# Pair sums of weighed states on GpSimd in a fused two-layer kernel on one core

## The chip, the cores and the metric

The kernel runs on one core of a Trainium2 chip. The time is device microseconds (us) of one launch, as the median of several runs. A core has TensorE (matmuls into PSUM banks of 128 x 512 f32), VectorE, ScalarE (activation functions), GpSimd (which works on SBUF only here) and SyncE, which issues the DMAs. Each engine runs its own list of instructions in order and waits on semaphores that others raise.

## The reference

There are eight batches of 512 tokens x 256 features and two layers. The first layer (attention-like mixing and a mixture of experts) isn't touched by the change. The second layer is a Mamba-like state-space block and a gated MLP with ternary weights. What matters of it:

```python
raw, gate = split(x @ W_in)                    # 512 inner features each
h  = silu(causal_conv4(raw) + conv_b)
ts, B, C = split(h @ W_x, [64, 80])            # 16 values of B and of C per token
dt = softplus(ts @ W_dt + b_dt)
dA = exp(dt[..., None] * A)                    # 16 states n per feature
state = dA * state + dt * B * h                # along the 512 tokens
y  = sum over n of state[n] * C[n]             # the sum that the change touches
y  = (y + h * D) * silu(gate);  out = y @ W_out
# then the MLP: silu(x@w1)*(x@w2) -> gelu(@h1) -> gelu(@h2) -> @w3, 1024 wide
```

## The kernel before

Features lie over the 128 partitions, the 512 tokens along the free axis. A batch's inner features are 4 tiles (`KI`), worked off in two halves of 2 tiles (`HC`). For each half the 16 states n are gone through, and for each n both tiles: one step s handles one (n, tile) pair, 64 steps (`STEPS`) a batch. The four steps of two successive states are 2n, 2n+1 (state n, tiles 0 and 1) and the two behind them.

One step is this chain:

- SyncE brings the rows of B and C for state n into `bc`, spread over the partitions (L1165, one DMA of 512 KB for two steps, three buffers).
- ScalarE writes exp(dt * A) into a PSUM bank (L1251; three banks, `DEC`; it waits until the step three before has been weighed).
- GpSimd multiplies `u` = dt * h by the row of B into `d_in` (L1186, three buffers, `IN`).
- VectorE scans along the tokens in the PSUM bank (L1196, `scan`), and behind the next scan it multiplies the state by the row of C into `w_st` (L1204, `weigh`; three buffers, `WG`; it waits until the step three before has been summed).
- TensorE adds the weighed state to the output's bank with the identity as the other operand (L1271). f32 matmuls show as two records each. The bank was begun with h * D (L1263).

After a half's last step VectorE multiplies the bank by the gate (L1210, `gate_output`), then TensorE does `W_out` (L193) and VectorE adds the result to the tokens, through the tile `tokB` (L1235, L1238).

Three things run beside each other in a period: the core of batch b, the front of batch b+1 (norm L181, `W_in`, convolution taps L1020 and L1024 on `raw` and `cv`, SiLU, dt; `front_*`), and the MLP of batch b-1 (`mlp_*`). The MLP's activations are kept as a high part in fp32r and a low part: ScalarE writes the Gelu twice (L1456), GpSimd subtracts (L1373, `f0L`, `f1L`), TensorE multiplies both parts (L199, L200), and VectorE does the gating of the first layer (L1394, L1398). The weights come by DMA into `w_stage` and are cast by ScalarE into `w_ring` (L1427). Exp, Gelu and SiLU need different activation tables on ScalarE, and every change of table is an `ACT_TABLE_LOAD`.

The order on each engine is set when the program is built: each part is a generator that gives a planned time before each piece (`step_at(b, s)` is 2.8 planned us a step, with offsets from the table `PLAN`), and `in_order` takes the piece with the smallest one. These are places in an order and not measured times.

## Time and profile before

| | us |
|---|---|
| median of 3 runs (lowest to highest) | 2847.69 (2846.69 to 2848.17) |
| profiled execution | 2851.47 |
| its span in the profile | 2849.6 |

| engine | busy us | share of the span |
|---|---|---|
| TensorE (PE) | 2498.0 | 88% |
| VectorE (DVE) | 1770.3 | 62% |
| ScalarE (ACT) | 1453.9 | 51% |
| GpSimd (POOL) | 1093.9 | 38% |

The shares are of the whole span, of which the first layer fills somewhat less than the first 1100 us. The rows on which the prediction rests are cut by batches: the scans of the eight batches begin at 1159.8, 1315.8, 1517.3, 1720.6, 1926.9, 2129.1, 2331.0 and 2535.2 us, and the last one ends at 2704.8. PE's ends are modelled, so a busy PE isn't PE at its peak; PEld is the weight load, which overlaps the matmuls. A wait is named by the engine, its output tile and line, and behind the arrow by what ended it.

### The profile page before, as it was taken

To read this page: it belongs to the slowest core of one execution; us is meant where nothing else is said; L and a number is where in the kernel's file an instruction comes from. 1 tells how busy PE (TensorE), PEld (TensorE's weight loads), DVE (VectorE), ACT (ScalarE), POOL (GpSimd) and SP (SyncE) were. 2 spreads that over 40 slices of the span, in tenths; PEclk is the share of its full clock that TensorE was granted. 3 is DMA by queue.
4 is the path that set the end of the run, shared out by engine and by line. 5 is a ranking of instruction groups with operands and counts; after the bars stand their busy time and mean duration, and the time that the engine had idled before them with its cause. 6 is when DMAs were issued, how large, how long until landed. Compare 5 with 4: busy or idle time off the path is not lost.

```text
span 2849.6 us, 25916 instructions
## 1 busy us (share of the span) xinstructions
PE 2498.0 (88%) x8180; PEld 1510.3 (53%) x8180; DVE 1770.3 (62%) x2758; ACT 1453.9 (51%) x1938; POOL 1093.9 (38%) x841
## 2 busy tenths in 40 slices
PE   2899999999999997677898898898898897998977
PEld 1456555565656564223555465465564564565665
DVE  2544444444444423789968869869779679678630
ACT  0222322323222222554686786786776776867733
POOL 0220101202010100455655565565565556557622
PEclk6899999999999998788999999999999999999989
DMA  7000000000000000344464564564554554546622
GB/s 250 0 0 1 23 23 0 23 1 23 1 23 6 3 8 30 104 117 116 134 173 126 136 178 113 140 171 111 148 159 124 164 146 125 162 140 164 173 76 82
DMA packets 278665, 263.33 MB, mean 92 GB/s; under 512 B 15136, under 2 KB 209456, under 8 KB 278528
## 3 DMA queue, kind: packets, MB, share of 16 engines
q1 hardware_dynamic: 278528, 261.67, 32.9%
q8 instruction: 66, 1.08, 0.2%
q14 instruction: 71, 0.58, 0.1%
HBM read 252.61 MB, written 9.01 MB: 92 GB/s over the span
## 4 chain that ended last, share of the span: by engine, by line
PE 18%; DVE 12%; issue 10%; ACT 8%; DMA 7%; POOL 4%; SPq 1%; DVEq 0%; ACTq 0%; POOLq 0%
DMA w_stage<-h_T 6%; PE bank L1271 5%; PE bank L193 4%; DVE w_st L1204 3%; DVE bank L1196 3%; PE bank L199 3%; PE bank L200 3%; POOL d_in L1186 2%; ACT w_ring L1427 2%; ACT bank L1251 2%; DVE cv L1024 2%; ACT L1251 2%; PE bank L1504 1%; POOL f1L L1373 1%; PE bank L1505 1%
## 5 line engine op out<-in xcount | busy, mean ns | idle before, releaser
L1186 POOL TENSOR_TENSOR d_in<-u,bc 128x512 f32<-128x512 f32 x512 | 665.3, 1315 | 444.6 <-DMA bc<-bc_rows 318.8
L1196 DVE TENSOR_TENSOR_SCAN bank<-bank,d_in 128x512 f32<-128x512 f32 x512 | 624.7, 1221 | 188.0 <-ACT bank L1251 159.7
L1271 PE MATMUL bank<-w_st,ident 128*128 128x512 f32 x1024 | 542.6, 643 | 118.7 <-DVE w_st L1204 118.4
L1251 ACT ACTIVATE bank<-dt,a_neg 128x512 f32<-128x512 f32 x512 | 348.1, 687 | 300.0 <-DVE w_st L1204 298.5
L199 PE MATMUL bank<-f1H,w_ring 128*128 128x512 f32 x768 | 355.5, 463 | 39.4 <-POOL f1L L1373 26.4
L1271 PEld LDWEIGHTS bank<-w_st,ident 128*128 128x128 f32 x1024 | 194.3, 201 | 351.3 <-DVE w_st L1204 222.8
L1204 DVE TENSOR_TENSOR w_st<-bank,bc 128x512 f32<-128x512 f32 x512 | 344.1, 673 | 55.1 <-PE bank L1271 54.9
L200 PE MATMUL bank<-f1L,w_ring 128*128 128x512 f32 x768 | 312.6, 407 | 0.0
L748 DVE SCALAR_TENSOR_TENSOR f_both<-bank,rt,f_both 128x256 f32<-128x256 f32 x256 | 112.1, 480 | 303.9 <-PE bank L193 303.9
L176 POOL TENSOR_TENSOR norm_rstd<-norm_veps,minus_half 128x4 f32<-128x4 f32 x24 | 24.3, 1011 | 613.3 <-DVE norm_veps L172 613.3
L199 PE MATMUL bank<-f0H,w_ring 128*128 128x512 f32 x512 | 227.9, 445 | 10.8 <-POOL f0L L1373 5.6
L797 ACT ACTIVATE e_act<-bank 128x512 f32<-128x512 f32 x128 | 75.7, 597 | 315.0 <-PE bank L193 314.8
L1427 ACT ACTIVATE w_ring<-w_stage 128x1024 fp32r<-128x1024 f32 (+1 forms) x192 | 173.1, 906 | 113.9 <-DMA w_stage<-h_T 57.6
L193 PE MATMUL bank<-w_down,e_act 128*128 128x256 f32 x1024 | 230.2, 379 | 0.0
L193 PE MATMUL bank<-f_both,w_up 128*128 128x512 f32 x512 | 228.9, 592 | 0.0
L1373 POOL TENSOR_TENSOR f0L<-mid,f0H 128x512 fp32r<-128x512 f32 x128 | 170.8, 1336 | 136.6 <-ACT f0H L1456 79.5
L193 PEld LDWEIGHTS bank<-w_down,e_act 128*128 128x128 f32 x1024 | 194.6, 190 | 50.3 <-issue 25.1
L199 PEld LDWEIGHTS bank<-f1H,w_ring 128*128 128x128 f32 x768 | 151.7, 198 | 111.9 <-issue 44.1
L200 PE MATMUL bank<-f0L,w_ring 128*128 128x512 f32 x512 | 206.2, 403 | 0.0
L200 PEld LDWEIGHTS bank<-f1L,w_ring 128*128 128x128 f32 x768 | 151.7, 198 | 52.5 <-issue 23.5
L193 PEld LDWEIGHTS bank<-f_both,w_up 128*128 128x128 f32 x512 | 97.3, 190 | 101.5 <-issue 98.8
L1251 ACT ACT_TABLE_LOAD x115 | 147.5, 1283 | 2.0
(175 smaller groups left out, 3573.6 us busy)
## 6 DMA issues: line engine op xcount, KB each, us to landing
bc<-bc_rows SPq DMA_DIRECT2D x256, 512.0 KB, 5.1
w_stage<-h_T SPq DMA_DIRECT2D x256, 256.0 KB, 3.4
w_stage<-w_T SPq DMA_DIRECT2D x128, 128.0 KB, 3.2
xA<-L_attn_x SPq DMA_DIRECT2D x8, 512.0 KB, 4.0
x_mid<-xA SPq DMA_DIRECT2D x8, 512.0 KB, 2.9
xB<-x_mid SPq DMA_DIRECT2D x8, 512.0 KB, 5.0
xM<-x_mid SPq DMA_DIRECT2D x8, 512.0 KB, 8.0
x_out<-xM SPq DMA_DIRECT2D x8, 512.0 KB, 6.6
```

Source lines behind the costliest of these rows:

```text
L193: i = pe.matmul(out_, lhs(k), rhs(k), start=(k == 0), stop=(k == nk - 1))
L199: pe.matmul(out_, weights(k), hi(k), start=(k == 0), stop=False)
L200: i = pe.matmul(out_, weights(k), lo(k), start=False, stop=(k == nk - 1))
L748: i = dve.scalar_tensor_tensor(out=f[:, t, :], in0=bank[:, j * D:(j + 1) * D], scalar=r[:, 7, t, e:e + 1], in1=f[:, t, :], op0=ALU.mult, o ...
L797: act.activation(e_act[:, e % 2, m, :], bank[:, :], ACT.Gelu).then_inc(up_act.sem, 1)
L1186: pool.tensor_tensor(d_in[:, nth(b, s) % IN, :], u[:, c, :], rows_tile(b, use)[:, 0, :], ALU.mult).then_inc(in_made.sem, 1)
L1196: dve.tensor_tensor_scan(bank[:, :], bank[:, :], d_in[:, nth(b, s) % IN, :], 0.0, ALU.mult, ALU.add).then_inc(scanned.sem, 1)
L1204: dve.tensor_tensor(w_st[:, nth(b, s) % WG, :], state_bank(b, s)[:, :], rows_tile(b, step(s)[2])[:, 1, :], ALU.mult).then_inc(weighed.sem, 1)
L1251: act.activation(state_bank(b, s)[:, :], dt[:, c, :], ACT.Exp, scale=a_neg[:, c, n:n + 1]).then_inc(dA_made.sem, 1)
L1271: pe.matmul(y_bank(c)[:, :], ident[:, :], w_st[:, nth(b, s) % WG, :], start=False, stop=(n == NST - 1)).then_inc(summed.sem, 1)
L1373: pool.tensor_tensor(lo, f_full[:, i % 2, :], hi.bitcast(F32), ALU.subtract).then_inc(low_made.sem, 1)
L1427: act.activation(ring_part(w), stage_part(w), ACT.Copy).then_inc(ring_made.sem, 1)
```

## The change

For a step of an odd state n, GpSimd adds the tile of the state before (same feature tile) to this one's in place (`pairs_pool`, new signal `paired`), and TensorE sums only the result: 256 sums in place of 512. `w_st` has four buffers (`2 * HC`) in place of three. The weighing waits for `paired` in a step of an even state and for `summed` in one of an odd state. The tile `tokB` goes and its rows lie in the convolution's `raw`, so ScalarE's copy of the first channel waits for the end of the batch two before. The table `PLAN` has new numbers.

```diff
 PLAN = dict(
-    rows_out=106.9, norm_rstd=29, norm_stats=26, norm_apply=34.2, conv=45.7, raw_gap=11.7, tap_gap=3, u_first=136.5,
+    pair=4.8, rows_out=106.9, norm_rstd=29, norm_stats=24.1, norm_apply=34.5, conv=45.1, raw_gap=11.7, tap_gap=3.2,
...
-            tokB = sb("tokB", [P, 2, D])
...
+            tokB = raw[:, 0, PAD:].rearrange("p (t d) -> p t d", d=D)
...
-            BC, IN, WG, DEC = 3, 3, 3, 3
+            BC, IN, WG, DEC = 3, 3, 2 * HC, 3
...
+            def weighed_tile(b, s):
+                return w_st[:, nth(b, s) % WG, :]
+
+            def pair(s):
+                return s // (2 * HC) * HC + s % HC
...
                         act.wait_ge(*tap_made.at(b - 1, (c + 3) * KC))
+                        if b >= 2 and c == 0:
+                            act.wait_ge(*xM_made.all(b - 2))
...
+            def pairs_pool(b):
+                for s in range(STEPS):
+                    if step(s)[0] % 2:
+                        yield step_at(b, s) + PLAN["pair"]
+                        pool.wait_ge(*weighed.at(b, s + 1))
+                        pool.tensor_tensor(weighed_tile(b, s), weighed_tile(b, s), weighed_tile(b, s - HC), ALU.add
+                                           ).then_inc(paired.sem, 1)
...
                     if nth(b, s) >= WG:
                         before, old = step_back(b, s, WG)
-                        dve.wait_ge(*summed.at(before, old + 1))
-                    dve.tensor_tensor(w_st[:, nth(b, s) % WG, :], state_bank(b, s)[:, :], rows_tile(b, step(s)[2])[:, 1, :], ALU.mult
+                        freed = summed if step(s)[0] % 2 else paired
+                        dve.wait_ge(*freed.at(before, pair(old) + 1))
+                    dve.tensor_tensor(weighed_tile(b, s), state_bank(b, s)[:, :], rows_tile(b, step(s)[2])[:, 1, :], ALU.mult
                                       ).then_inc(weighed.sem, 1)
 
                 def gate_output(c):
-                    dve.wait_ge(*summed.at(b, (c // HC + 1) * HALF))
+                    dve.wait_ge(*summed.at(b, (c // HC + 1) * HALF // 2))
...
-                    pe.wait_ge(*weighed.at(b, s + 1))
-                    pe.matmul(y_bank(c)[:, :], ident[:, :], w_st[:, nth(b, s) % WG, :], start=False, stop=(n == NST - 1)
-                              ).then_inc(summed.sem, 1)
+                    if n % 2:
+                        pe.wait_ge(*paired.at(b, pair(s) + 1))
+                        pe.matmul(y_bank(c)[:, :], ident[:, :], weighed_tile(b, s), start=False, stop=(n == NST - 1)
+                                  ).then_inc(summed.sem, 1)
```

On GpSimd, in the full batch that the trace shows from 1720.6 us on, from step 42 to step 50 (`d_in` the product of each step, `f1L` and `f0L` the MLP's low halves), before:

```order
L1186 TENSOR_TENSOR d_in<-u,bc 128x512 x4
L1373 TENSOR_TENSOR f1L<-mid,f1H 128x512
L1186 TENSOR_TENSOR d_in<-u,bc 128x512
L1373 TENSOR_TENSOR f1L<-mid,f1H 128x512
L1186 TENSOR_TENSOR d_in<-u,bc 128x512 x4
L1373 TENSOR_TENSOR f0L<-mid,f0H 128x512
```

The same stretch of GpSimd now, steps 43 to 51 (`w_st<-w_st` is the addition):

```order
L1195 TENSOR_TENSOR d_in<-u,bc 128x512 x3
L1203 TENSOR_TENSOR w_st<-w_st 128x512
L1195 TENSOR_TENSOR d_in<-u,bc 128x512
L1203 TENSOR_TENSOR w_st<-w_st 128x512
L1392 TENSOR_TENSOR f1L<-mid,f1H 128x512
L1195 TENSOR_TENSOR d_in<-u,bc 128x512
L1392 TENSOR_TENSOR f1L<-mid,f1H 128x512
L1195 TENSOR_TENSOR d_in<-u,bc 128x512 x2
L1203 TENSOR_TENSOR w_st<-w_st 128x512
L1195 TENSOR_TENSOR d_in<-u,bc 128x512
L1203 TENSOR_TENSOR w_st<-w_st 128x512
L1195 TENSOR_TENSOR d_in<-u,bc 128x512
```

The addition of step s stands behind the product of step s+3, and the low halves are one step later than they were.

On TensorE, at that batch's end, where the output's bank is closed (the dt tiles of the next batch, then the last sums), before:

```order
L193 MATMUL bank<-xp,w_dt 128x512 x2
L1271 MATMUL bank<-w_st,ident 128x512 x3
L1504 MATMUL bank<-w,f0H 128x256
L1505 MATMUL bank<-w,f0L 128x256
L1504 MATMUL bank<-w,f0H 128x256
```

The same place on TensorE now:

```order
L193 MATMUL bank<-xp,w_dt 128x512 x2
L1290 MATMUL bank<-w_st,ident 128x512 x2
L1523 MATMUL bank<-w,f0H 128x256
L1524 MATMUL bank<-w,f0L 128x256
L1523 MATMUL bank<-w,f0H 128x256
```

Two sums stand between the dt tiles and the MLP's last products where there were three.

## Rows read from the trace of the kernel before

**Rows 1.** Busy us by stretch: PE, PEld, DVE, ACT, POOL, PEclk, DMA share, GB/s.

```profile
1160.00:1316.00 156.00, 111.83 (x192) 38.83 (x192) 138.46 (x166) 75.89 (x105) 87.33 (x67) 0.82 0.44 115
1721.00:1927.00 206.00, 180.36 (x619) 112.03 (x618) 163.81 (x204) 150.15 (x193) 118.09 (x92) 0.96 0.53 142
2535.00:2705.00 170.00, 155.56 (x549) 100.51 (x548) 135.88 (x170) 125.90 (x160) 108.03 (x86) 0.96 0.61 163
```

**Rows 2.** The same by stretches of one batch, and 21 steps of the last.

```profile
1720.60:1819.60 99.00, 79.44 (x279) 48.22 (x278) 96.29 (x128) 61.66 (x80) 54.20 (x41) 0.93 0.46 119
1819.60:1863.50 43.90, 41.59 (x135) 24.66 (x134) 24.80 (x30) 37.98 (x49) 22.55 (x18) 1.00 0.55 148
1863.50:1917.90 54.40, 50.63 (x177) 33.92 (x176) 39.38 (x45) 42.06 (x53) 35.65 (x30) 0.97 0.65 184
1917.90:1926.90 9.00, 9.00 (x36) 5.54 (x35) 3.63 (x7) 8.74 (x13) 5.70 (x5) 1.00 0.40 117
2649.10:2703.50 54.40, 50.97 (x178) 34.14 (x177) 37.30 (x43) 43.07 (x54) 35.45 (x29) 0.97 0.60 173
```

**Rows 3.** Waits of 1721 to 1927: total us, times, longest us.

```profile
POOL d_in L1186 <- DMA bc<-bc_rows: 39.5, 13, 5.6
...
DVE bank L1196 <- ACT bank L1251: 23.5, 9, 5.4
...
POOL f1L L1373 <- ACT f1H L1456: 14.6, 4, 5.2
...
DVE w_st L1204 <- PE bank L1271: 8.2, 6, 2.7
...
POOL f0L L1373 <- ACT f0H L1456: 7.1, 4, 3.4
...
DVE hcv L1210 <- PE bank L1271: 6.4, 2, 5.4
```

**Rows 4.** The chain that ended last, 1517 to 2535, shares by line.

```profile
by line: issue 17.0%; DMA w_stage<-h_T 10.5%; PE bank L1271 7.6%; DVE bank L1196 6.5%; DVE w_st L1204 6.3%; PE bank L199 5.1%; PE bank L193 4.9%; PE bank L200 4.9%; ACT bank L1251 3.2%; ACT L1251 2.9%; POOL d_in L1186 2.8%; ACT w_ring L1427
```

**Rows 5.** One piece of the chain in 1721 to 1927: start us, us.

```profile
1885.17 2.58 PE bank L1271 x6
```

**Rows 6.** Timeline at a batch's end: start us, us, then idle before it.

```profile
1922.80 2.84 PE L1271 MATMUL bank<-w_st,ident 128*128 128x512 f32 x6
...
1925.68 1.29 DVE L1210 TENSOR_TENSOR hcv<-bank,gate 128x512 f32<-128x512 f32 x2 [5.37 <-PE bank L1271]
```

**Rows 7.** Single lines over the whole run: ns least/median/most, first and last start.

```profile
L1024 DVE SCALAR_TENSOR_TENSOR cv<-raw,conv_w,cv x96: 729/750/1867, 1127.6 to 2435.3; 128x512 f32<-128x512 f32 x96
...
L1398 DVE CAST f0H<-mid x64: 404/450/1503, 1360.5 to 2753.5; 128x512 fp32r<-128x512 f32 x64
...
L181 DVE TENSOR_SCALAR cv<-xB,normB_stat,normB_rstd x32: 400/1348/1492, 1118.4 to 2372.0; 128x256 f32<-128x256 f32 x32
L181 DVE TENSOR_SCALAR mid<-xM,normM_stat,normM_rstd x32: 398/407/1368, 1339.5 to 2729.9; 128x256 f32<-128x256 f32 x32
...
L1196 DVE TENSOR_TENSOR_SCAN bank<-bank,d_in x512: 1205/1219/1232, 1159.8 to 2703.5; 128x512 f32<-128x512 f32 x171
...
L1204 DVE TENSOR_TENSOR w_st<-bank,bc x512: 665/673/694, 1162.1 to 2705.3; 128x512 f32<-128x512 f32 x171
...
L1186 POOL TENSOR_TENSOR d_in<-u,bc x512: 1254/1282/2239, 1158.5 to 2701.7; 128x512 f32<-128x512 f32 x171
...
L1251 ACT ACT_TABLE_LOAD  x115: 1283/1283/1283, 1155.9 to 2697.8; - x115
```

**Rows 8.** Groups of VectorE in 1721 to 1927: busy us, mean ns.

```profile
L1024 DVE SCALAR_TENSOR_TENSOR cv<-raw,conv_w,cv 128x512 f32<-128x512 f32 x12 | 12.6, 1048 | 0.0
L1398 DVE CAST f0H<-mid 128x512 fp32r<-128x512 f32 x8 | 6.3, 785 | 0.1
...
L181 DVE TENSOR_SCALAR cv<-xB,normB_stat,normB_rstd 128x256 f32<-128x256 f32 x4 | 4.4, 1151 | 0.0
L181 DVE TENSOR_SCALAR mid<-xM,normM_stat,normM_rstd 128x256 f32<-128x256 f32 x4 | 3.7, 976 | 0.0
```

More of the change, by code:

```diff
@@ L915, in adaln_kernel @@
             y_begun = signal("y_begun", KI)
-            dA_made, in_made, scanned, weighed, summed = (signal(n, STEPS) for n in
-                                                          ("dA_made", "in_made", "scanned", "weighed", "summed"))
+            dA_made, in_made, scanned, weighed = (signal(n, STEPS) for n in ("dA_made", "in_made", "scanned", "weighed"))
+            paired, summed = signal("paired", STEPS // 2), signal("summed", STEPS // 2)
             y_gated = signal("y_gated", KI)
@@ L1511, in adaln_kernel @@
                      *(mlp_sync(b) for b in every), *(out_sync(b) for b in every))
-            in_order(*(front_pool(b) for b in every), *(core_pool(b) for b in every), *(mlp_pool(b) for b in every))
+            in_order(*(front_pool(b) for b in every), *(core_pool(b) for b in every), *(pairs_pool(b) for b in every), *(mlp_pool(b) for b in every))
             in_order(*(front_scalar(b) for b in every), *(core_scalar(b) for b in every), *(weights_scalar(b) for b in every),
```

12 lines of the change are left out of this document (6 added, 6 removed).

## The prediction

> **What bounds the kernel now.** I read the busy times by stretch first, then the waits, then the chain, then single durations. The first layer holds none of the changed code. What the change can move are the eight state cores between 1160 and 2705 us: the first, 156 us, beside the second batch's front only, six full periods of about 203 us, (2535 - 1316) / 6, and the last, 170 us, with no front beside it [rows 1]. The 145 us behind them, to the span's 2849.6, are the last MLP, which the change leaves as it is.
>
> In a full period (206 us in the one shown) TensorE is busy 180.4 us, VectorE 163.8, ScalarE 150.2 and GpSimd 118.1. TensorE has the largest share, but the period is not one stage. Cut at scans 0, 30, 42 and 63 it reads [rows 2]: over the first 99 us VectorE is busy 96.3 and TensorE 79.4, so the first half of a batch, with norms, convolution and the gating of the MLP's first layer, is VectorE's. In the next 43.9 us TensorE has 41.6 and ScalarE 38.0 while VectorE has 24.8. In the 54.4 us after that TensorE shows 50.6 and ScalarE 42.1. But the last core, with less other work on TensorE before it, also takes 54.4 us for the same 21 states, so that stretch keeps a cadence of its own. It is the ring of exponentials (three PSUM banks) broken by ScalarE's Gelu groups: VectorE waits 23.5 us a batch for an exponential, against 8.2 us in the weighing for a sum by TensorE and 6.4 us in the gating of the output [rows 3]. The chain that ended last says the same of five periods (1018 us): the sums, L1271, hold 7.6% of it, and VectorE's scans and weighings 12.8% [rows 4].
>
> **The change part by part.**
>
> *TensorE loses every second sum.* 256 of 512 matmuls with the identity go. A matmul is two records; three of them took 2.84 us with the tail of the last, and 2.58 in the chain, so 0.86 us each [rows 5, 6]. That is 220 us of TensorE's time, 27.5 a batch. Only what VectorE waits for counts of it. The weighing L1204 waits 8.2 us a batch for one of three buffers. Now a buffer is one of four: an odd state's tile must be summed four states later, not three, and an even state's is freed by GpSimd and not by TensorE, which sits for two hidden tiles in a row. I let 7 of the 8.2 us go. At the batch's end VectorE waits 5.37 us before the gating while TensorE does two dt tiles and three sums [rows 6]; now there are two sums, 0.86 us less. With the 1.0 us at the first half's end (the rest of the 6.4) I take 2 us.
>
> *GpSimd gains 32 additions a batch.* The nearest row is its own product of the same shape, d_in, 1.28 us in the median [rows 7]: 41 us a batch, 118 to 159 of 203. The order puts the addition of state s behind d_in of s+3, two additions to four products. With nothing else to do, VectorE takes 1.22 + 0.67 us for a state, 7.6 for four [rows 7], and GpSimd 6 x 1.28 = 7.7: equal. In the cadence of scans 42 to 63, 2.6 us a state, GpSimd is busy 35.7 of 54.4 us; 10.5 additions make it 49. So it keeps up, but its stretches of waiting (39.5 us a batch for the row DMAs, 14.6 and 7.1 for the Gelu halves [rows 3]) shrink to a fifth of the time. The added wait is the weighing of an even state behind the addition of the state two before it. Behind that weighing on VectorE stand the next scan and everything else, and ScalarE's exponential three states on waits for it. Its slack is two states less the addition, some 2 us. I take 1 us a batch for it; below, 0, if GpSimd is always in time, and above, all that the first rival gives.
>
> *The additions get in VectorE's way.* Of VectorE's operations some stretch while GpSimd runs: the convolution's taps L1024 took 729 ns at least and 1867 at most, the cast L1398 404 to 1503, the normalisation L181 398 or 400 to 1368 and 1492, while the scan stayed within 1205 to 1232 and the weighing within 665 to 694 [rows 7]. In the period shown the excess over the shortest is 12 x 0.32 = 3.8 us for L1024, 4 x 0.75 + 4 x 0.58 = 5.3 for L181, 8 x 0.38 = 3.0 for L1398 [rows 7, 8], together 12.1 us, nearly all in the 99 us in which VectorE has no idle time to hide it. GpSimd is busy 54.2 of these 99 us [rows 2]; 15 additions are 19.2 us more, 35%. So 12.1 x 0.35 = +4.3 us a batch. Below it could be 0 (the additions fall beside scans), above 12.1 again if every one of them hits.
> By the Trainium skill (GPSIMD Engine Reference, Key points) GpSimd shares its SBUF interfaces with VectorE and contends with VectorE instructions that run in a two-port mode or have two SBUF inputs. The trace agrees on the operations that stretch (L1024 has two SBUF inputs) and on the weighing and scan, which read one from PSUM and do not. If one counted by the rule each addition that meets such an instruction as a full block of 1.28 us, and all 15 met one, the stretch would lose 19 us in place of 4.3, and the whole would come out 55 us later than my sum; the 12.1 us over 28 operations, 0.43 each, say that a third of a block is met on the average. It is the far end of the third rival below.
>
> *The order.* Between the same scans stands nearly the same work as before, one or two states later. ScalarE loads 12 activation tables fewer over the program, at 1.28 us [rows 7], three a batch in most batches: two of them where VectorE is the bound, worth nothing, and one between scans 40 and 42, where VectorE waits for ScalarE: -1.3 us a batch. SyncE's queue is as before but for one weight tile that passes the output's store, cost nothing. The token rows in the convolution's buffer add a wait of the copy of batch b's first channel for the token rows of b-2, which are due 25 us of planned time earlier (places 17.6 and 42.3): nothing; VectorE writes them in its own order, after the last tap that reads the buffer.
>
> **The sum** for a full period: -7 - 2 + 1 + 4.3 - 1.3 = -5.0 us of 203. Six of them are -30. The last core has no front beside it, hence less of each term: -3. The first has no MLP beside it, and TensorE is busy 111.8 of 156 us: 0. That is -33 from the profiled execution's own 2851.47 us (its span of 2849.6 and 1.9 around it), 2818.5. It ran 3.8 us over the median of the runs, so 2815 for the median.
>
> **The rivals.**
> *TensorE is the real bound from scan 30 on.* For: 41.6 of 43.9 and 50.6 of 54.4 us busy, the highest share of all engines. Against: VectorE waits only 14.6 us a batch for it, and the last core's 54.4. Then 17 sums a batch, 14.6 us, come off whole, with -1.3 and +4.3: -11.3 a period, -68 for six, -13 for the last core with less contention: 2847.7 - 81 = about 2766. The chain's 7.6% of 1018 us, 77 us in five periods, halved, is 7.7 us a period and lies between this and my 9 us for the two waits together.
> *GpSimd becomes the pace, and the kernel slower.* It works in order, and an MLP half that waits for a Gelu holds up the addition behind it, which holds the weighing, hence the exponential. Between scans 30 and 63 (98.3 us) it is busy 58.2 [rows 2]; 16.5 additions make 79.4. If it still waits the 21.7 us for the Gelu halves, it needs 101.1: 2.8 us more a period, none of the 9 us won, contention as above: +7 a period, +43 and +5 for the last core: about 2896. It decides from 18.9 us of such waits on. Against: in the new order the additions of the states before stand ahead of the halves, and the waits are partly GpSimd being early.
> *The waits only change their name.* The 8.2 us go over to the additions in greater part (3 us won), the gating wins 1, contention doubles to 8: about +3 us, with the table load +2 a period or none: 2848 to 2860.
> *TensorE's clock.* It was granted at 0.93 of its upper level in the VectorE-bound stretch and 0.82 over the first core, where TensorE had pauses, and at 0.97 to 1.00 in the rest of the period [rows 1, 2]. At 0.90 in place of the period's 0.96 the 153 us that TensorE keeps would grow by 10, which the 27.5 us taken off cover. It widens the range and is no case of its own.
>
> **How the numbers follow.** Forecast 0.47; TensorE bound 0.20; GpSimd's pace 0.18; waits renamed 0.15. I call 0.2%, 5.7 us, the least that can be told from no change. Faster: 0.46 of the forecast's, 0.20, and 0.03 of the last case: 0.69. Same: 0.01 and 0.09: 0.10. Slower: 0.18 and 0.03: 0.21. The likeliest case alone spans 2790 to 2835 (contention 0 to 8 us, waits won 5 to 11). The range goes down to the TensorE case, 2760, and up to where GpSimd's pace is only partly reached, 2872.
>
> **What would show it.** Right: the waits of L1204's successor for TensorE near 1 us a batch and a new wait for the addition of 1 to 2 us; the stretch of scans 0 to 30 some 3 to 5 us longer with longer taps and casts; scans 30 to 42 shorter by 5 or so; 42 to 63 within 2 us of 54.4; GpSimd busy near 159 us a period. Wrong: a VectorE wait for the addition of over 5 us a batch (GpSimd's pace), a period under 195 us (TensorE was the bound), taps that did not lengthen, or an exponential's wait that grew by what the others lost.

## The result and the profile after

The changed kernel takes 2906.38 us (median of 4 runs, 2902.64 to 2914.07) against 2847.19 us (2845.11 to 2848.17) for the kernel before: a ratio of 1.0212, 95% interval 1.019 to 1.0234. It is slower by 59 us, where 2815 us and a gain of 33 were forecast. The profiled execution took 2914.07 us with a span of 2912.3, 62.7 over the span before.

Where the 62.7 us lie, by the starts of the scans: the first core takes 161.1 us (156.0 before), the six full periods from 1320.6 to 2584.2 take 1263.6 (1219.4), the last core 179.6 (168.3), and behind the last scan come 148.5 (146.1). That is 5.1 + 44.2 + 11.3 + 2.4, less 0.3 at the start. A full period is 210.6 us where it was 203.2.

The stretches of one batch after, answering to [rows 2], columns as there: scans 0 to 30, 30 to 42, 42 to 63, 63 to the next batch's first, and 21 steps of the last core.

```profile
1740.50:1840.90 100.40, 73.73 (x263) 47.68 (x262) 99.82 (x127) 59.15 (x79) 73.81 (x55) 0.88 0.49 117
1840.90:1881.80 40.90, 36.63 (x118) 22.35 (x116) 24.11 (x29) 36.35 (x47) 29.11 (x23) 0.96 0.56 159
1881.80:1941.90 60.10, 45.25 (x147) 31.60 (x147) 41.15 (x45) 42.59 (x54) 50.33 (x41) 0.83 0.56 166
1941.90:1951.70 9.80, 9.10 (x31) 5.11 (x31) 3.61 (x5) 8.19 (x12) 8.66 (x7) 1.00 0.41 107
2704.00:2763.80 59.80, 51.05 (x169) 35.70 (x168) 39.37 (x44) 46.63 (x59) 52.28 (x43) 0.88 0.57 165
```

In the first stretch VectorE is fuller than it was (99.8 of 100.4 us, where it was 96.3 of 99.0), and the stretch is 1.4 us longer. The middle stretch is shorter by 3.0. The third, for 21 states, is 5.7 longer, and in it TensorE (45.3 of 60.1 us) and VectorE (41.2) both have room; the engine whose busy time rose is GpSimd, 35.7 to 50.3 us. One batch scatters by a few us, so here are the means over the six full periods, from the scan starts of each trace; I use them for all kernels below. The last column is VectorE's busy time between the first scan of the second batch and the first scan of the last one, divided by six.

| us, mean of six periods | period | scans 0-30 | 30-42 | 42-63 | 63-next | VectorE busy |
|---|---|---|---|---|---|---|
| before | 203.2 | 96.2 | 43.2 | 55.0 | 8.8 | 161.5 |
| after | 210.6 | 99.5 | 42.5 | 58.8 | 9.8 | 167.1 |

So of +7.4 a period, 3.3 lie in the VectorE-bound half, 3.8 in scans 42 to 63, 1.0 between scan 63 and the next batch, and the middle gives back 0.7. In scans 0 to 30 VectorE is busy 98.6 us in the mean, where it was 93.7.

Now the same time by what VectorE did. Busy times over the same five batches, before and then after (columns as in [rows 1]):

```profile
1517.00:2535.00 1018.00, 906.54 (x3081) 562.55 (x3081) 807.90 (x1016) 750.12 (x961) 592.48 (x460) 0.95 0.53 143
```

```profile
1532.00:2584.00 1052.00, 818.13 (x2759) 527.32 (x2759) 837.72 (x1016) 736.47 (x950) 805.42 (x620) 0.89 0.51 139
```

VectorE issues the same 1016 instructions, is busy 29.8 us longer for them, and idle 214.3 us in place of 210.1. TensorE is busy 88 us less, and VectorE's idle time didn't fall at all. The waits over the five batches, before:

```profile
POOL d_in L1186 <- DMA bc<-bc_rows: 185.9, 66, 6.1
ACT bank L1251 <- DVE w_st L1204: 166.8, 142, 4.0
DVE bank L1196 <- ACT bank L1251: 113.9, 44, 5.4
...
POOL f1L L1373 <- ACT f1H L1456: 74.5, 20, 5.6
...
DVE w_st L1204 <- PE bank L1271: 38.8, 26, 2.7
...
POOL f0L L1373 <- ACT f0H L1456: 37.6, 20, 3.9
...
DVE hcv L1210 <- PE bank L1271: 33.9, 10, 5.4
...
DVE bank L1196 <- POOL d_in L1186: 9.9, 7, 2.0
```

And after, where L1213 is the scan, L1222 the weighing, L1228 the gating, L1195 the product, L1203 the addition and L1290 the sum:

```profile
ACT bank L1269 <- DVE w_st L1222: 236.0, 152, 6.7
...
POOL d_in L1195 <- DMA bc<-bc_rows: 107.2, 52, 8.0
DVE bank L1213 <- ACT bank L1269: 100.7, 36, 6.4
PE bank L1290 <- POOL w_st L1203: 87.3, 44, 6.4
...
POOL w_st L1203 <- DVE w_st L1222: 60.3, 23, 4.7
...
DVE bank L1213 <- POOL d_in L1195: 43.2, 37, 4.5
DVE hcv L1228 <- PE bank L1290: 40.9, 10, 6.2
DVE w_st L1222 <- PE bank L1290: 24.9, 10, 5.0
...
POOL f1L L1392 <- ACT f1H L1475: 21.0, 15, 2.7
...
POOL f0L L1392 <- ACT f0H L1475: 1.5, 3, 1.2
```

The weighing's wait for TensorE fell by 13.9 us and not by 35 (7 a batch); the gating's rose by 7.0; and there is a wait that the prediction never priced, the scan's for GpSimd's product, 9.9 to 43.2. The wait that it did price, of the weighing for the addition, does not appear here; over the whole run the trace has 0.2 us of it. TensorE and not VectorE waits for the addition.

Not all of the 43.2 us are the additions' doing. A good part of them are waits at scans 40 and 60 for a product that had itself stood waiting for its rows. At scan 60 the kernel before has that wait too; at scan 40 it doesn't. The place in the batch shown (timeline: start us, us, idle before it; SPq is SyncE's queue, L1364 a weight tile, L1174 the rows of B and C):

```profile
1864.30 0.92 SPq L1364 DMA_DIRECT2D w_stage<-h_T  x2
1865.26 0.51 SPq L1174 DMA_DIRECT2D bc<-bc_rows  x1
...
1871.95 2.54 POOL L1195 TENSOR_TENSOR d_in<-u,bc 128x512 f32<-128x512 f32 x2 [6.43 <-DMA bc<-bc_rows]
...
1873.28 1.23 DVE L1213 TENSOR_TENSOR_SCAN bank<-bank,d_in 128x512 f32<-128x512 f32 x1 [4.02 <-POOL d_in L1195]
```

The weighing that frees the rows' buffer (step 35) ended at 1861.0 us, but SyncE issued the rows at 1865.3 only: it stood 7.5 us in front of the weight tile ahead of them, waiting for ScalarE's cast. In the six full batches these rows are issued 4.3 to 8.3 us behind that weighing, and 0.6 to 0.7 us behind it in the kernel before. The kernel without additions in the new order, below, has the same wait, and the one in the old order has not (10.2 us of waits for products in five batches), so it comes with the order.

The gating at the end of the batch shown, answering to [rows 6], waits 6.17 us where it waited 5.37:

```profile
1950.50 1.29 DVE L1228 TENSOR_TENSOR hcv<-bank,gate 128x512 f32<-128x512 f32 x2 [6.17 <-PE bank L1290]
```

The chain of the same stretch, answering to [rows 4]:

```profile
by line: issue 23.2%; DVE bank L1213 9.2%; POOL d_in L1195 8.2%; DVE w_st L1222 6.5%; DMA w_stage<-h_T 5.9%; POOL w_st L1203 5.3%; DMA bc<-bc_rows 5.3%; PE bank L199 3.6%; PE bank L200 3.3%; DVE cv L1031 2.6%; DVE mid L1413 2.6%; POOL f1L L
```

The sums have all but left it and GpSimd has come in: the product had 2.8% and has 8.2%, the addition has 5.3%, and the row DMAs, which had no part in it over the same batches before, have 5.3%.

Single operations of the whole run, ns least/median/most, answering to [rows 7]: the taps, the cast, the addition, the product, the scan and the weighing.

```profile
L1031 DVE SCALAR_TENSOR_TENSOR cv<-raw,conv_w,cv x96: 731/752/1915, 1127.9 to 2479.4; 128x512 f32<-128x512 f32 x96
```

```profile
L1417 DVE CAST f0H<-mid x64: 405/884/1499, 1367.0 to 2814.7; 128x512 fp32r<-128x512 f32 x64
```

```profile
L1203 POOL TENSOR_TENSOR w_st<-w_st x256: 1254/1282/2286, 1169.7 to 2767.0; 128x512 f32<-128x512 f32 x128
```

```profile
L1195 POOL TENSOR_TENSOR d_in<-u,bc x512: 1256/1278/2266, 1158.2 to 2762.5; 128x512 f32<-128x512 f32 x171
```

```profile
L1213 DVE TENSOR_TENSOR_SCAN bank<-bank,d_in x512: 1205/1219/1232, 1159.5 to 2763.8; 128x512 f32<-128x512 f32 x171
```

```profile
L1222 DVE TENSOR_TENSOR w_st<-bank,bc x512: 664/673/693, 1161.8 to 2765.6; 128x512 f32<-128x512 f32 x171
```

The addition costs what the product costs, as taken. The cast's median went from 450 to 884 ns: in the typical case it now meets GpSimd. Scans and weighings are as they were.

### The profile page after: what moved, and what is told of

Read it like the earlier page. It is cut to its first block, busy times and chain, and to the rows that moved or that the text cites. A ratio compares the mean times of both kernels' runs of the same rounds, so it can differ in the third digit from the quotient of the medians.

```text
span 2912.3 us, 25135 instructions
## 1 busy us (share of the span) xinstructions
PE 2360.4 (81%) x7668; PEld 1456.9 (50%) x7668; DVE 1810.7 (62%) x2758; ACT 1439.2 (49%) x1926; POOL 1428.5 (49%) x1097
## 4 chain that ended last, share of the span: by engine, by line
DVE 15%; issue 14%; POOL 12%; PE 8%; DMA 7%; ACT 5%; SPq 0%; DVEq 0%; POOLq 0%; ACTq 0%
POOL d_in L1195 6%; DVE bank L1213 5%; DMA w_stage<-h_T 4%; POOL w_st L1203 4%; DMA bc<-bc_rows 3%; DVE w_st L1222 3%; PE bank L199 2%; PE bank L200 2%; PE bank L193 2%; DVE cv L1031 2%; POOL f1L L1392 1%; PE bank L1290 1%; ACT w_ring L1446 1%; DVE mid L1413 1%; DVE mid L181 1%
## 5 line engine op out<-in xcount | busy, mean ns | idle before, releaser
L1195 POOL TENSOR_TENSOR d_in<-u,bc 128x512 f32<-128x512 f32 x512 | 667.8, 1312 | 229.1 <-DMA bc<-bc_rows 161.4
L1213 DVE TENSOR_TENSOR_SCAN bank<-bank,d_in 128x512 f32<-128x512 f32 x512 | 624.6, 1221 | 219.1 <-ACT bank L1269 141.6
L1290 PE MATMUL bank<-w_st,ident 128*128 128x512 f32 x512 | 320.8, 726 | 206.4 <-POOL w_st L1203 206.3
L199 PE MATMUL bank<-f1H,w_ring 128*128 128x512 f32 x768 | 365.5, 476 | 74.7 <-DVE mid L1413 26.1
L1203 POOL TENSOR_TENSOR w_st<-w_st 128x512 f32<-128x512 f32 x256 | 347.4, 1357 | 88.3 <-DVE w_st L1222 88.0
L1222 DVE TENSOR_TENSOR w_st<-bank,bc 128x512 f32<-128x512 f32 x512 | 343.8, 673 | 39.0 <-PE bank L1290 36.2
L200 PE MATMUL bank<-f1L,w_ring 128*128 128x512 f32 x768 | 330.7, 431 | 0.0
L1290 PEld LDWEIGHTS bank<-w_st,ident 128*128 128x128 f32 x512 | 99.4, 218 | 331.5 <-POOL w_st L1203 292.7
L199 PEld LDWEIGHTS bank<-f1H,w_ring 128*128 128x128 f32 x768 | 164.3, 214 | 170.4 <-issue 97.8
L193 PEld LDWEIGHTS bank<-w_down,e_act 128*128 128x128 f32 x1024 | 194.6, 190 | 50.3 <-issue 25.1
L200 PE MATMUL bank<-f0L,w_ring 128*128 128x512 f32 x512 | 213.3, 417 | 0.0
L200 PEld LDWEIGHTS bank<-f1L,w_ring 128*128 128x128 f32 x768 | 163.9, 213 | 50.2 <-issue 16.6
L577 POOL TENSOR_TENSOR qk_tok<-qk_tok,os_row_t 128x512 f32<-128x512 f32 x32 | 53.5, 1700 | 212.7 <-DVE qk_tok L526 212.7
```

The source lines that it names most:

```text
L193: i = pe.matmul(out_, lhs(k), rhs(k), start=(k == 0), stop=(k == nk - 1))
L199: pe.matmul(out_, weights(k), hi(k), start=(k == 0), stop=False)
L200: i = pe.matmul(out_, weights(k), lo(k), start=False, stop=(k == nk - 1))
L1195: pool.tensor_tensor(d_in[:, nth(b, s) % IN, :], u[:, c, :], rows_tile(b, use)[:, 0, :], ALU.mult).then_inc(in_made.sem, 1)
L1203: pool.tensor_tensor(weighed_tile(b, s), weighed_tile(b, s), weighed_tile(b, s - HC), ALU.add).then_inc(paired.sem, 1)
L1213: dve.tensor_tensor_scan(bank[:, :], bank[:, :], d_in[:, nth(b, s) % IN, :], 0.0, ALU.mult, ALU.add).then_inc(scanned.sem, 1)
```

## The experiments

Theory A: VectorE's waits belong to a ring of exponentials and weighings, so taking TensorE out of them only renames them, and the additions cost in two ways, by longer VectorE operations and by GpSimd's time in front of the products. Theory B: the new order is at fault. Theory C: the weighings or sums that wait for an addition are. The expectations call the additions' part of theory A theory G, theory B rival O and theory C rival W. All ratios are against the kernel before on the same chip; "us more" or "less" is against its median there (2848.9 to 2852.0).

### Which part costs: order, relief, additions

**The new order alone**, in the kernel before: the whole of the new `PLAN`, in which the sums' number is 6.8 (5.6 before).

```diff
 PLAN = dict(
...
-    hid_gap=13.8, mlp=20, up=14, hid=3.6, up_cast_even=-0.5, up_cast_odd=6.5, hid_cast_even=8, hid_cast_odd=12.6,
...
+    dt_pe_second=-5.4, gate_pe_second=16.6, rows_in=3.3, input=4.2, weigh=-10.6, out_add=13.6, decay=4, sum=6.8,
...
```

> The work of the kernel before, 512 sums and no additions, in the new order: only the table PLAN is the changed kernel's. Theory G (GpSimd: its additions hold up its own products, and they stretch VectorE's operations): the order alone costs little, 2840 to 2862 us, and scans 42 to 63 of a full batch stay near 54.5 us. Rival O (the new order is what costs, since the halves and products stand one or two states later): 2885 to 2910, scans 42 to 63 near 59 us.

Measured: 2936.74 us, ratio 1.0316 (1.0293 to 1.0339), outside both expectations. The longest wait of VectorE over five batches in that kernel:

```profile
DVE w_st L1204 <- PE bank L1271: 141.1, 48, 7.4
```

The new order puts the sums later behind the weighings; with 512 sums and three buffers the weighing waits 141.1 us for TensorE where it waited 38.8. With all 512 sums the new order is a loss; what it does with half of them the next runs show.

**The changed kernel in the old order**: the numbers of the kernel before, and the additions' own, 4.8, kept.

```diff
 PLAN = dict(
-    pair=4.8, rows_out=106.9, norm_rstd=29, norm_stats=24.1, norm_apply=34.5, conv=45.1, raw_gap=11.7, tap_gap=3.2,
...
+    pair=4.8, rows_out=106.9, norm_rstd=29, norm_stats=26, norm_apply=34.2, conv=45.7, raw_gap=11.7, tap_gap=3, u_first=136.5,
...
```

> The changed kernel with the old PLAN (the addition at its new place, 4.8). Theory G: as slow as the changed kernel or a little slower, 2900 to 2925. Rival O: 2850 to 2870.

Measured: 2976.72 us, 1.0454 (1.0432 to 1.0476), again outside both. So the new order is worth 70 us to the changed work, and theory B falls: without it the change would cost 128 us and not 59.

**The changed kernel without the additions** (TensorE sums the odd states' tiles only):

```diff
-                        freed = summed if step(s)[0] % 2 else paired
-                        dve.wait_ge(*freed.at(before, pair(old) + 1))
+                        if step(s)[0] % 2:
+                            dve.wait_ge(*summed.at(before, pair(old) + 1))
...
-                        pe.wait_ge(*paired.at(b, pair(s) + 1))
+                        pe.wait_ge(*weighed.at(b, s + 1))
...
-            in_order(*(front_pool(b) for b in every), *(core_pool(b) for b in every), *(pairs_pool(b) for b in every), *(mlp_pool(b) for b in every))
+            in_order(*(front_pool(b) for b in every), *(core_pool(b) for b in every), *(mlp_pool(b) for b in every))
```

> The changed kernel without GpSimd's additions: TensorE sums only the tiles of the odd states, the even states are left out of the output. It keeps the gain of the change (256 sums fewer) without its price. Theory G: below the kernel before by what VectorE waited for TensorE, about 9 us a period: 2785 to 2815, scans 0 to 30 near 96 us again and 42 to 63 at 50 to 54. Rival T (TensorE with fewer sums falls to its lower clock, and the hidden tiles behind it come late): 2850 to 2900, and the clock of scans 42 to 63 near 0.83 as in the changed kernel.

Measured: 2849.62 us, 1.0003 (0.9987 to 1.0019): no gain, with half the sums, four buffers and the order made for them, so the 9 us a period weren't there. Nor is rival T borne out: scans 42 to 63 take 54.9 us at a granted clock of 0.88 to 0.91. What the additions add in this order is the 57 us to the changed kernel. The scan's wait for a product, over five batches:

```profile
DVE bank L1213 <- POOL d_in L1195: 25.9, 14, 3.8
```

It was 9.9 us before, is 25.9 here without any addition (at scan 40, and longer than before at scan 60), and 43.2 in the changed kernel. So 16.0 of the 33.3 us come without additions and 17.3 with them.

**The same in the old order**: the diff just shown, with the old `PLAN`.

> No additions, and only the odd states' tiles summed (the even states are left out of the output), in the old order. It is the relief of TensorE alone. In the new order this took the time of the kernel before. If TensorE's relief is worth what VectorE waited for it, 9 us a period: 2785 to 2815. If nothing waits for TensorE in the end (the cadence is that of VectorE, ScalarE and the row DMAs): 2835 to 2850. If TensorE's lower clock takes it back: over 2850.

Measured: 2842.33 us, 0.997 (0.996 to 0.998): 7 us less, where the two terms for TensorE's waits made 54 over six periods. Its waits over five batches:

```profile
DVE bank L1213 <- ACT bank L1269: 156.9, 43, 6.2
...
POOL f1L L1392 <- ACT f1H L1475: 79.5, 20, 5.3
...
DVE hcv L1228 <- PE bank L1290: 29.8, 10, 6.7
PE bank L199 <- POOL f0L L1392: 28.6, 5, 6.0
PE bank L199 <- POOL f1L L1392: 26.1, 5, 5.2
```

The weighing's 38.8 us are gone (the line has no row left), and the exponential's wait has grown from 113.9 to 156.9, by 43.0. On TensorE 54.7 us of waits for GpSimd's low halves stand where there were 15.8: the time won there is spent waiting for what follows the Gelus. That is the renaming, shown in the old order. In the changed kernel the new order sums later, and there the weighing's wait mostly stayed (24.9 us).

**The additions alone**: the kernel before, 512 sums, and 32 additions of constants a batch at the places of the new ones, for which nobody waits. It has the token rows in the convolution's buffer, to make room for the additions' own tile: with `tokB` kept beside it, the tile `mid` wants 8192 bytes a partition and 7296 are left. Each addition waits only for the addition before it, which writes the same tile.

```diff
+            def spare_pool(b):
+                for s in range(STEPS):
+                    if step(s)[0] % 2:
+                        yield step_at(b, s) + 4.8
...
+                        pool.tensor_tensor(spare[:, :], w_in[:, 0, 0:S], w_in[:, 1, 0:S], ALU.add).then_inc(spare_made.sem, 1)
```

> The kernel before, in its own order with its 512 sums, and 32 GpSimd additions a batch at the changed kernel's places. They read constant weights and write a tile that nothing reads; nobody waits for them (the token rows lie in the convolution's rows to make room). Theory G (GpSimd's time and its meeting with VectorE are the price): 2900 to 2935. Rival W (the price is the waits for the additions): 2850 to 2875.

Measured: 2939.82 us, 1.0305 (1.0283 to 1.0327): 91 us more, for work that no instruction waits for. That is a little over the 2900 to 2935 expected, and theory C isn't needed for a loss of that size.

Together:

| median us | old order | new order |
|---|---|---|
| the kernel before's work | 2848 | 2937 |
| half the sums, no additions | 2842 | 2850 |
| half the sums, additions | 2977 | 2906 |
| all sums, unawaited additions | 2940 | |

### How the additions cost

**Unawaited additions in the new order.** The kernel without additions, with the constants' additions in the place of the real ones; two tiles of `w_st` take turns for the odd states, one serves the even ones, one is the additions' own. An even weighing waits for the weighing before it here, which VectorE has done earlier in its own order anyway; I take that wait as free, and no run tests it.

```diff
             def weighed_tile(b, s):
-                return w_st[:, nth(b, s) % WG, :]
+                return w_st[:, 1 + s % HC if step(s)[0] % 2 else 0, :]
+            spare = w_st[:, 3, :]
...
+                        pool.tensor_tensor(spare, w_in[:, 0, 0:S], w_in[:, 1, 0:S], ALU.add).then_inc(spare_made.sem, 1)
```

> The kernel without additions in the new order (2850 us), plus additions at their places that read constants, write a spare tile and are waited for by nobody (the even states are left out of the output). Theory G: 2890 to 2906, nearly all of the changed kernel's 2906. Rival W: 2850 to 2865, and the rest up to 2906 is the waits for the additions.

Measured: 2937.32 us, 1.0307 (1.0286 to 1.0328), 31 us more than the changed kernel itself and above both expectations. In this order, to free the additions and their readers from waiting saves nothing.

**A small operation in their place**: the same kernel, each addition replaced by a 128x4 power, the operation of the norms.

```diff
-                        pool.tensor_tensor(spare, w_in[:, 0, 0:S], w_in[:, 1, 0:S], ALU.add).then_inc(spare_made.sem, 1)
+                        pool.tensor_tensor(spare[:, 0:TT], sc_in[:, 0, 0:TT], minus_half[:, :], ALU.pow).then_inc(spare_made.sem, 1)
```

> As the one before, with each addition replaced by a power of a 128 x 4 tile, which took 1.01 us in the trace of before and moves almost no data (the even states are left out of the output). GpSimd is busy nearly as long, but hardly touches its memory interface. If the meeting with VectorE's taps, casts and norms is the price: near 2855, with the taps at their length of the kernel before. If GpSimd's time in its order is the price: 2880 to 2895.

Measured: 2876.19 us, 1.0088 (1.0068 to 1.0108), near the lower end of the second expectation. The group of the power, and that of the additions in the kernel before this one (GpSimd; busy us, mean ns, idle before):

```profile
L1206 POOL TENSOR_TENSOR w_st<-sc_in,minus_half 128x4 f32<-128x4 f32 x256 | 275.1, 1075 | 0.1
```

```profile
L1206 POOL TENSOR_TENSOR w_st<-w_in 128x512 f32<-128x512 f32 x256 | 354.4, 1384 | 0.1
```

The power holds GpSimd for 78% as long and moves hardly any data. It costs 27 us over the kernel without additions; the additions cost 88. Of the 61 us between, most lies where VectorE is full: it is busy 159.4 us a period here and 168.4 with the additions, and scans 0 to 30 take 93.9 and 101.1, which is 43 us in six periods. The first and the last core take some 6 us more each with the additions. What the shorter occupation, 79 us of GpSimd in the whole run, has in it wasn't told apart.

**Each half by itself**: the additions alone, in steps 0 to 31 only, then in steps 32 to 63 only, then the second half with the power.

```diff
-                    if step(s)[0] % 2:
+                    if step(s)[0] % 2 and s < 32:       # then: and s >= 32
```

> The kernel before with additions that nobody waits for in steps 0 to 31 alone (16 a batch, reading constants, tokens in the convolution's rows). Where VectorE is the bound, an addition costs what it stretches VectorE's taps, norms and casts by. By the phases of the run with all 32, scans 0 to 30 took 5 us a period of its 11: 2880 to 2900. If the first half's share is mere occupation, which VectorE's bound would hide: under 2865.

> The same additions in steps 32 to 63 alone. Theory G (they hold up products and MLP halves in GpSimd's order, where VectorE has idle time to take any stretching): 2880 to 2900. If the second half's share came over from the first through late work: under 2865.

> As the one before with powers of a 128 x 4 tile in the additions' places, which hardly touch the memory interface and take about 1.05 us in place of 1.4. If GpSimd's time is what the second half pays: 2870 to 2885, three quarters of the additions' cost or more. If the meeting with VectorE is: under 2860.

Measured: 2898.62 us, 1.0164 (1.014 to 1.0187); 2894.40, 1.0149 (1.0118 to 1.0179); 2888.53, 1.0138 (1.0115 to 1.0161). The last is above the 2870 to 2885 expected. The first two, +50 and +46, add up to about the 91 of both. And they are not the same cost. Means of six periods:

| us | period | scans 0-30 | 30-42 | 42-63 | 63-next | VectorE busy |
|---|---|---|---|---|---|---|
| before | 203.2 | 96.2 | 43.2 | 55.0 | 8.8 | 161.5 |
| additions, first half | 208.8 | 101.3 | 43.9 | 54.8 | 8.9 | 169.2 |
| additions, second half | 209.4 | 97.8 | 43.4 | 59.2 | 9.0 | 163.8 |
| power, second half | 208.2 | 98.0 | 43.4 | 58.1 | 8.7 | 162.8 |

With the additions in the first half VectorE is busy 7.7 us a period longer, and the period is 5.6 longer, 5.1 of them in scans 0 to 30, where VectorE has hardly any idle time to give. (Six periods make 34 of the 50 us; the last core takes 11 more.) With the additions in the second half it is busy 2.3 us longer, the period is 6.2 longer, and 4.2 of them are in scans 42 to 63. The power, with 1.3 us of VectorE's time, still costs 40 us where the additions cost 46 (their intervals overlap): there it is GpSimd's time, for the most part. The place, in the kernel with additions in the second half (timeline of VectorE, GpSimd and ScalarE: start us, us, idle before it; L1189 the product, L1197 the addition, L1206 the scan, L1214 the weighing, L1383 the low half, L1466 the Gelu):

```profile
1713.31 1.22 DVE L1206 TENSOR_TENSOR_SCAN bank<-bank,d_in 128x512 f32<-128x512 f32 x1
...
1714.43 0.68 DVE L1214 TENSOR_TENSOR w_st<-bank,bc 128x512 f32<-128x512 f32 x1
...
1715.27 0.68 ACT L1466 ACTIVATE f0H<-bank,sc_in 128x512 fp32r<-128x512 f32 x1
...
1716.03 1.30 POOL L1383 TENSOR_TENSOR f0L<-mid,f0H 128x512 fp32r<-128x512 f32 x1 [2.98 <-ACT f0H L1466]
...
1717.28 1.31 POOL L1197 TENSOR_TENSOR spare<-w_in 128x512 f32<-128x512 f32 x1
...
1718.54 1.28 POOL L1189 TENSOR_TENSOR d_in<-u,bc 128x512 f32<-128x512 f32 x1
...
1719.85 1.23 DVE L1206 TENSOR_TENSOR_SCAN bank<-bank,d_in 128x512 f32<-128x512 f32 x1 [4.74 <-POOL d_in L1189]
```

GpSimd stands 2.98 us in front of a low half whose Gelu isn't there; then it does the half, the addition and at last the product, for which VectorE has waited 4.74 us. The wait of scans for products is 49.5 us over five batches in this kernel, 9.9 before. The same place costs 4 to 5 us at scan 61 of the full batches. The changed kernel, in its new order, doesn't have it: its low halves hardly wait (1.5 us in five batches for `f0L`).

### Cures that were tried

**The addition earlier** (`pair=2.0` for 4.8 in the changed kernel's `PLAN`).

> The changed kernel with the addition one product earlier in GpSimd's order (pair=2.0 in place of 4.8: behind the product of step s+2). GpSimd then stands waiting for the weighing with the next product behind it. Theory G (the product that is held up in GpSimd's order is the price): slower than the changed kernel, 2920 to 2960, with VectorE's wait for GpSimd above the 8.6 us a period of the changed kernel. If only the meeting on the memory interface counts: 2900 to 2912.

Measured: 2947.59 us, 1.0349 (1.0307 to 1.0392), 41 us more than the changed kernel. GpSimd waits 178.0 us over five batches for weighings, where it was 60.3, and the scans wait 66.6 for a product, where it was 43.2. What waits on GpSimd holds the products behind it.

**Pairs only in steps 28 to 39**, where VectorE has room, in the old order, all other tiles summed singly.

```diff
+            def paired_with(s):
+                first = s // (2 * HC) * 2 * HC
+                if not (28 <= first < 40):
+                    return None
+                return s + HC if s - first < HC else s - HC
```

> The kernel before in its own order, with pairs only in steps 28 to 39 (6 additions a batch, 58 sums), where both VectorE and TensorE were not held by additions and the changed kernel won 1 to 2 us a period; the tokens lie in the convolution's rows and there are four buffers of weighed states. If the relief is worth something where TensorE is fullest: 2830 to 2843. Theory G with a relief worth nothing: 2848 to 2862 (91 us for 32 additions a batch, 6 of them about 15).

Measured: 2862.05 us, 1.0035 (1.0018 to 1.0052). Six additions a batch, with their 6 sums fewer, cost 10 us.

**A fourth product buffer**, beside the power.

```diff
-            BC, IN, WG, DEC = 3, 3, 2 * HC, 3
+            BC, IN, WG, DEC = 3, 4, 2 * HC, 3
...
-            spare = w_st[:, 3, :]
+            spare = sb("spare", [P, TT])
```

> The kernel with the powers in the additions' places (2876 us; the even states are left out of the output), with four buffers of products d_in in place of three. The powers cost 27 us over the kernel without them by GpSimd's time alone. If that is because the products come late, a fourth buffer lets GpSimd run a step further ahead: 2850 to 2864. If not (the products' rows by DMA, or the MLP's halves, are what comes late): 2870 to 2880.

Measured: 2873.14 us, 1.0081 (1.0055 to 1.0107), not told from the 1.0088 with three. The waits of the scans for a product fell by 7.5 us over five batches (49.5 to 42.0) and the time didn't follow.

**Is the ring of exponentials the bound before?** The kernel before, with the first of each Gelu's two writes cut from 512 to 8 columns, 16 a batch.

```diff
-                    for part in (f_full[:, i % 2, :], (f1H, f0H)[layer][:, m, :]):
+                    for part, n in ((f_full[:, i % 2, 0:8], 8), ((f1H, f0H)[layer][:, m, :], S)):
```

> The kernel before with the first of the two Gelus of a hidden tile cut to 8 of 512 columns (the low parts are wrong): 16 a batch, some 6 to 7 us of ScalarE's time, at places where it holds up the exponentials. Theory R (the pace of a batch's second half is the ring of exponentials on ScalarE and scans on VectorE): 2800 to 2822. If TensorE or the weights' DMAs were the pace there: 2838 to 2850.

Measured: 2831.82 us, 0.9929 (0.9909 to 0.9948). The write's median fell from 688 to 267 ns, 16 x 0.42 = 6.7 us a batch, 54 us in eight, of which 20 came back. That lies between the two expectations. The wait for exponentials fell from 113.9 to 80.2 us over five batches. A microsecond off ScalarE is worth 0.37 us here. Half the sums in the old order took 146 us off TensorE's busy time (2498.0 to 2351.6 over the run) and brought 7, or 0.05 each.

## Why the prediction was wrong

**What bounds the kernel: half right.** Scans 0 to 30 are VectorE's: what lengthens it there lengthens them. That 42 to 63 keep the cadence of ScalarE's ring is borne out in part: the shorter Gelu took 2.3 us off them and 2.6 off scans 30 to 42, though scans 0 to 30 grew by 1.6. I did not follow the two to their end: if the ring sets the cadence, a wait for TensorE within it is not there to be won.

**"I let 7 of the 8.2 us go", and 2 us at the gating: this step failed.** With half the sums and nothing else (old order) the kernel gains 7 us in all, where 54 were counted, while the exponential's wait grows by 43.0 us in five batches, more than the 38.8 that go. The text names this as a sign of error, and as a rival at 0.15. In the changed kernel the idle time of VectorE rose by 0.8 us a period where the terms for waits and tables (-7, -2, +1, -1.3) made -9.3. The relief itself was mis-sized too: with half the sums in the old order TensorE's busy time fell by 18.0 us a period and not by 27.5, while the granted clock of the six periods went from 0.95 to 0.89.

**"So it keeps up": this step failed.** GpSimd's load was right (161.9 us busy in the batch shown, about 159 forecast; additions 1357 ns in the mean against 1.28 us). The error was in which instruction is late. I priced the weighing behind the addition at 1 us a batch, and it is nothing. But GpSimd works in order, and behind the addition stand the products for the next scans. The scans' waits for them go from 9.9 to 43.2 us, 6.7 a period, of which 3.5 need the additions (25.9 without them in the same order). Scans 42 to 63 take 3.8 us more a period, forecast within 2. In the new order without additions they take 54.9, so there the additions are the whole of it: 2.6 of those 3.9 us a period are longer waits for products and 1.5 VectorE's own longer operations. With additions in the second half only, and no sum taken away, it is 4.2 there, and with the power, which is shorter and moves hardly any data, 40 of those 46 us are still paid.

**The contention, +4.3 us a period: right in kind and about in size.** The forecast was for scans 0 to 30. There VectorE is busy 4.9 us longer (93.7 to 98.6), and the stretch grew by 3.3, about 20 us in six periods, as its last idle time went; over the whole period VectorE is busy 5.6 us longer. With the additions there alone, in the old order, the stretch grew by 5.1.
The Trainium skill (GPSIMD Engine Reference, Key points) says that GpSimd's SBUF interfaces are shared with VectorE and that instructions of two SBUF inputs or in a two-port mode contend; the traces agree, and show both engines' instructions lengthened, as the last section shows. The far end that I worked out beside it, each addition a full block of 1.28 us, wasn't reached; its "55 us" is wrong besides, as 19 in place of 4.3 in six periods is 88.

**The table load, -1.3, and scans 30 to 42, "shorter by 5 or so":** the mean is shorter by 0.7 us. The 12 loads did go (287 to 275 in the traces); what one is worth by itself wasn't tried.

**The order, "nearly the same work as before, one or two states later": priced at nothing, wrong both ways.** It costs 88 us with the old work and saves 70 with the new. It moves the sums further behind the weighings, and with three buffers and 512 sums the weighings wait 102 us more in five batches. That the sums' number in `PLAN` is the one that does it is argued, not tried. And SyncE's queue, "as before but for one weight tile", cost something: the rows of scan 40 come late behind a weight tile, and in the first four full batches that scan waits for its product, 11.8 us in all without additions and 12.8 in the changed kernel, where it didn't wait before.

**The token rows in the convolution's buffer: right**, nothing. The kernels with half the sums have them too, and the one in the old order is faster than before.

**TensorE's clock: right** as no case of its own. It was granted 0.83 of its upper level in scans 42 to 63 of the batch shown (0.97 before, [rows 2]), where TensorE now pauses for additions. Over its span the changed kernel has 0.898 and the kernel before 0.941. The kernel with half the sums in the old order has 0.899 and is 7 us faster than the kernel before. I took that TensorE's remaining work would grow by 10 us a period at 0.90; in that kernel it is busy 162.4 us where 180.4 less 27.5 make 152.9.

**The first and last core** were taken as 0 and -3 and are +5.1 and +11.3. The additions are there too: GpSimd is busy 126.7 us in the first core (1160 to 1321 us) for 87.3 [rows 1], and 52.3 in the last 21 steps for 35.5 [rows 2].

**The rivals.** "GpSimd becomes the pace", 2896 us at 0.18, is the nearest to what happened. Its sum for scans 30 to 63 was 79.4 us busy and 101.1 us long; in the batch shown they are 29.11 + 50.33 = 79.4 busy and 101.0 long, mean over six periods 101.3. Its reason is only partly right: in the changed kernel the waits for Gelu halves have all but gone (74.5 to 21.0 and 37.6 to 1.5 us in five batches), and waits for the weighing (60.3) stand in their place. The sum had those 21.7 us a batch in it, and the trace has 4.5, so that its 101.1 us come out is in part luck. Its sign, a VectorE wait for the addition over 5 us, doesn't show; the wait has the product's name. What I held against it, that the order puts additions ahead of the halves, is true, and the new order, of which that is a part, saved 70 us of 128. "TensorE is the real bound", 2766 us at 0.20, falls with the two kernels of half the sums (2850 and 2842 us); its -11.3 should read -11.6. "The waits only change their name" names what became of the won waits, but not the cost of the additions in front of the products, and its 2848 to 2860 is missed.

**What stays open.** Why unawaited additions in the new order cost 31 us more than real ones. The two profiled executions differ by 19 us only. Six periods hold 21: VectorE is busy 1.3 us a period longer, and its gating waits 2.3 us a period longer for TensorE (52.4 against 40.9 us in five batches). Why it does isn't known. Awaited additions in the old order cost 37 us more than unawaited ones there. In that kernel GpSimd waits 136.2 us over five batches for weighings, and the scans wait 68.4 us for products against 48.3, which is the 4.0 us by which the period is longer; that the one makes the other is argued, not tried. So theory C isn't needed for the loss, but waits for the addition's input have a price in some orders.

## What to carry to other kernels

When an engine is to take over work, ask what stands behind the new instruction in its queue: here VectorE waited for the additions 0.2 us in all, but the next products stood behind them and the scans behind those. Look at the queues of the other engines in the new order too: the rows that came late behind a weight tile had nothing to do with the additions. A wait on a ring that another engine paces is not there to be won, and the test is cheap: drop the work without doing it elsewhere and see what name the wait takes. Don't take the idle time of an engine for room: GpSimd, at 59% in scans 30 to 63 before and 79% after, works in order and waits for rows, Gelus and weighings in between, and the additions had a price there.

## What the runs showed of the hardware

GpSimd and VectorE lengthen each other. A piece of the changed kernel, GpSimd and VectorE:

```profile
1899.35 1.30 POOL L1203 TENSOR_TENSOR w_st<-w_st 128x512 f32<-128x512 f32 x1
1899.93 1.80 DVE L1038 TENSOR_TENSOR dt<-dt,cv 128x1024 f32<-128x1024 f32 x1
...
1900.91 1.95 POOL L1195 TENSOR_TENSOR d_in<-u,bc 128x512 f32<-128x512 f32 x1 [0.27 <-DMA bc<-bc_rows]
...
1901.76 2.18 DVE L1043 TENSOR_TENSOR u<-dt,hcv 128x1024 f32<-128x1024 f32 x1
...
1902.83 2.29 POOL L1203 TENSOR_TENSOR w_st<-w_st 128x512 f32<-128x512 f32 x1
...
1903.87 1.22 DVE L1213 TENSOR_TENSOR_SCAN bank<-bank,d_in 128x512 f32<-128x512 f32 x1
...
1905.06 1.31 POOL L1195 TENSOR_TENSOR d_in<-u,bc 128x512 f32<-128x512 f32 x1
```

The two VectorE operations have two SBUF inputs each. `u` takes 2.18 us where its least is 1.22, the product beside it 1.95 and the addition 2.29 where theirs are 1.26 and 1.25; the scan, with one input in PSUM, takes its 1.22 beside the same addition. The ends tell more. The addition, `dt`, the product, `u` and the next addition end at 1900.65, 1901.73, 1902.86, 1903.94 and 1905.12 us, in turns, each 1.08 to 1.18 us behind the other engine's: about the least time of one. So each seems to have waited for the other to end and then run. I had counted only VectorE's side. Over the whole run scans and weighings, which read one input from PSUM, stayed within 27 and 29 ns of their least.

How long a GpSimd operation takes goes with its size: an addition of 128x1024 in the first layer of the kernel before took 2.35 us in the median and a product of 128x512 1.28. The power on 128x4 took 1.01 us, so it is dear for what it moves, and a good stand-in for occupation without data.
